# The attention stage of a one-core transformer kernel: new orders of the instructions on TensorE, VectorE, ScalarE, GpSimd and of the spreads

## The reference

```python
x = x + attn_a(_layernorm(x), ...)   # the stage that is changed
x = x + moe(_layernorm(x), ...)      # top 2 of 8 experts
x = x + gated_recurrence(_layernorm(x), ...)
x = x + moe(_layernorm(x), ...)

def attn_a(x):                        # 16 heads of 8, S = 256
    q, k, v = split(layernorm(x) @ in_proj_w.T + in_proj_b)
    scores = q @ k.T / sqrt(8) + causal_bias(rel_pos)
    x = x + (softmax(scores) @ v) @ out_w.T + out_b
    return x + relu(layernorm(x) @ w1.T + b1) @ w2.T + b2
```

## Time and profile before

| | |
|---|---|
| Three runs, median (lowest to highest) | 1711.88 us (1706.98 to 1714.66) |
| The profiled execution, its span | 1713.82 us, 1712.1 us |
| Busy over the span: PE, DVE, ACT, POOL | 1262.9, 1140.9, 965.3, 998.9 us |
| Mean granted TensorE clock (1 is 2.4 GHz) | 0.873 |

### The profile page before, as it was taken

The page is one execution under the profiler, slowest core; times in us unless marked ns, Lnnn a source line. Parts: engine busy times, 40 slices in busy tenths (PEclk is TensorE's granted clock), DMA queues, the critical chain, the costliest instruction groups (busy, mean ns, idle before and its releaser), DMA issues. The chain is left out here.

```text
span 1712.1 us, 37950 instructions
## 1 busy us (share of the span) xinstructions
PE 1262.9 (74%) x11717; PEld 1039.7 (61%) x11717; DVE 1140.9 (67%) x3828; ACT 965.3 (56%) x2002; POOL 998.9 (58%) x1152
## 2 busy tenths in 40 slices
PE   4688888888888888887458878747766628888750
PEld 2456666666666666665357878735554518878750
DVE  5377777777777777776555555548888735656548
ACT  2487877777777777775144444336666524444420
POOL 4234567767667667666745555534888845555450
PEclk8599999998999999988678998969899859999985
DMA  7121011111111111110332222211222122222218
GB/s 201 53 66 41 33 43 52 47 52 52 44 49 50 48 54 53 46 37 22 127 85 78 78 76 72 74 54 52 78 83 79 45 80 73 75 76 82 73 55 288
DMA packets 100818, 120.94 MB, mean 71 GB/s; under 512 B 17944, under 2 KB 80720, under 8 KB 100368
## 3 DMA queue, kind: packets, MB, share of 16 engines
q1 hardware_dynamic: 69600, 75.85, 14.9%
q0 software_dynamic: 17280, 35.95, 6.2%
q10 hardware_dynamic: 13744, 6.75, 1.4%
HBM read 49.45 MB, written 44.46 MB: 55 GB/s over the span
## 5 line engine op out<-in xcount | busy, mean ns | idle before, releaser
L1096 DVE TENSOR_TENSOR ebuf<-score_banks,region 128x768 f32<-128x768 f32 x256 | 243.9, 953 | 150.2 <-PE score_banks L809 143.7
L1333 ACT ACTIVATE region<-ebuf 128x768 f32<-128x768 f32 x256 | 216.9, 847 | 38.9 <-DVE ebuf L1096 34.8
L1311 ACT CAST copied<-max_banks 128x768 bf16<-128x768 f32 x256 | 204.7, 800 | 58.8 <-PE max_banks L797 55.8
L1745 POOL DMA_INDIRECT choice_rows<-first_yo,first_xg x142 | 137.3, 967 | 130.3 <-DVE first_yo L1865 96.3
L1745 POOL DMA_INDIRECT choice_rows<-second_yo,second_xg x142 | 137.1, 965 | 126.5 <-DVE second_yo L1865 92.3
L2161 POOL DMA_INDIRECT expert_rows<-d_rows,z_d_index x128 | 130.0, 1016 | 39.2 <-issue 31.9
L1614 POOL DMA_INDIRECT expert_rows<-d_rows,a_d_index x128 | 135.8, 1061 | 27.0 <-issue 21.3
L1821 ACT ACTIVATE first_silu<-first_bgu,first_biases 128x256 f32<-128x256 f32 x142 | 63.3, 477 | 130.1 <-PE first_bgu L1774 50.9
L1821 ACT ACTIVATE second_silu<-second_bgu,second_biases 128x256 f32<-128x256 f32 x142 | 62.9, 477 | 129.6 <-issue 52.2
L774 PE MATMUL max_banks<-identb,region 128*128 128x128 bf16 x512 | 109.8, 236 | 18.9 <-ACT copied L1311 17.7
L1857 DVE SCALAR_TENSOR_TENSOR first_hT<-first_bgu,first_biases,first_silu 128x256 f32<-128x256 f32 x142 | 64.3, 478 | 81.3 <-ACT first_silu L1821 49.1
(11 more groups left out here) (333 smaller groups left out, 4487.7 us busy)
## 6 DMA issues: line engine op xcount, KB each, us to landing
region_r<-region_r SPq DMA_DIRECT2D x192, 128.0 KB
first_xg<-expert_rows SPq DMA_DIRECT2D x71, 132.0 KB
second_xg<-expert_rows SPq DMA_DIRECT2D x71, 132.0 KB
z_rows<-choice_rows SPq DMA_DIRECT2D x32, 256.0 KB
c_rows<-choice_rows SPq DMA_DIRECT2D x16, 512.0 KB
out<-xres ACTq DMA_DIRECT2D x16, 256.0 KB
choice_rows<-first_yo,first_xg POOLq DMA_INDIRECT x142
choice_rows<-second_yo,second_xg POOLq DMA_INDIRECT x142
```

Of the source, the lines that this page charges most:

```text
L1096: nc.vector.tensor_tensor(ebuf[:, half_of_ebuf(c, j), :, :], score_banks[:, :, 0:BK], bias32[:, plain(j), :], ALU.add).then_inc(scores_fre ...
L1311: nc.scalar.copy(copied[:, 2 * j:2 * j + 2, :], max_banks[:, :, 0:BK]).then_inc(maxed_free, 1)
L1333: nc.scalar.activation(p32[:, j % 4, :, :], ebuf[:, half_of_ebuf(c, j), :, :], ACT.Exp).then_inc(exped, 1)
L1745: pool.indirect_dma_start(choice_dram, bass.IndirectOffsetOnAxis(ap=xg[:, i % G, t, E:E + 1].bitcast(I32), axis=0), yo[:, i % 4, t, :], No ...
```

## The change

No operation is added, removed or resized. The calls in the five body functions stand in another order, and some of them work on another batch in a given body: on DVE the third fold, masks 5 to 7, and the second norm of a batch now open the next body, on ACT exponentials 6 and 7, on POOL row_apply, the second root, second_apply, residuals, normed and normed_input come one body later and the roots one body earlier in the numbering. FIRST goes from -3 to -4 for that. In W_USES rank comes ahead of up. The DVE function second_norm is split into second_sum and second_norm; waits of DVE for its own statistics move from the end of one function to the start of the next (marks). On SP spread_projected is split into the upper and the lower parts of q and k, so q's are issued before k's. The diff, without the renamed arguments and the calls of body:

```diff
-    FIRST, FULL = -3, 8
+    FIRST, FULL = -4, 8
     T_USES = {"xmT": 2, "ot": 1, "up": 2, "row": 4, "oT": 1, "max": -1, "project": -3}
-    W_USES = {"project": -2, "ot": 1, "up": 2, "router": 4, "norm": -3, "rank": 5, "att": 1, "down": 2}
+    W_USES = {"project": -2, "ot": 1, "rank": 5, "up": 2, "router": 4, "norm": -3, "att": 1, "down": 2}
...
-            def body(b, n):
-                after, before = (n + 1) % RING, (n - 1) % RING
-                fill(b, n, 0, b + 1, after, 3)
-                weigh(b - 1, before, 3)
+            def body(b):
+                fill(b, b % RING, 0, b + 1, (b + 1) % RING, 3)
                 mlp_down(b - 3, 1)
-                fill(b, n, 1, b + 1, after, 4)
+                weigh(b - 1, (b - 1) % RING, 3)
+                fill(b, b % RING, 1, b + 1, (b + 1) % RING, 4)
+                project_kv(b + 2)
                 mlp_T(b - 2)
-                project_kv(b + 2)
-                fill(b, n, 2, b + 1, after, 5)
+                fill(b, b % RING, 2, b + 1, (b + 1) % RING, 5)
                 turn(b - 1)
-                fill(b, n, 3, b + 1, after, 6)
+                fill(b, b % RING, 3, b + 1, (b + 1) % RING, 6)
+                weigh(b, b % RING, 0)
+                rank(b - 5)
                 mlp_up_1(b - 2)
+                fill(b, b % RING, 4, b + 1, (b + 1) % RING, 7)
                 mlp_up_0(b - 2)
-                fill(b, n, 4, b + 1, after, 7)
                 row_T(b - 4)
-                weigh(b, n, 0)
+                fill(b, b % RING, 5, b + 2, (b + 2) % RING, 0)
                 router(b - 4)
-                fill(b, n, 5, b + 2, before, 0)
                 out_T(b - 1)
+                weigh(b, b % RING, 1)
                 norm_T(b + 3)
-                weigh(b, n, 1)
-                rank(b - 5)
-                fill(b, n, 6, b + 2, before, 1)
+                fill(b, b % RING, 6, b + 2, (b + 2) % RING, 1)
                 out_proj(b - 1)
-                max_T(b + 1, after)
+                max_T(b + 1)
+                weigh(b, b % RING, 2)
+                fill(b, b % RING, 7, b + 2, (b + 2) % RING, 2)
+                mlp_down(b - 2, 0)
                 project_q(b + 3)
-                fill(b, n, 7, b + 2, before, 2)
-                weigh(b, n, 2)
-                mlp_down(b - 2, 0)
 
...
-                    ch.mark(nc.vector.bn_stats(stats[:, t, :], tile(c, t)))
-                ch.wait(ch.base + ch.n)
+                    marks["norm"] = ch.mark(nc.vector.bn_stats(stats[:, t, :], tile(c, t)))
...
-            def second_norm(c, n):
+            def second_sum(c, n):
...
+
+            def second_norm(c):
+                if not exists(c):
+                    return
                 dve.wait_ge(W_free, useW("att", c) + 1)
                 for t in range(2):
-                    last = ch.mark(nc.vector.bn_stats(stats2[:, t, :], y1[:, t, :]))
-                ch.wait(last)
+                    marks["second"] = ch.mark(nc.vector.bn_stats(stats2[:, t, :], y1[:, t, :]))
...
+                ch.wait(marks["second"])
...
-            def body(b, n):
-                after, before = (n + 1) % RING, (n - 1) % RING
+            def body(b):
+                fold_keys(b, 2)
+                fold_half(b, 2)
+                fold_on(b, P // 4)
+                add_mask(b - 1, 5)
+                fold_on(b, P // 8)
+                sort(b - 5)
+                reduce_max(b, P // 8)
+                number(b - 5)
+                add_mask(b - 1, 6)
+                second_sum(b - 2, (b - 2) % RING)
+                second_norm(b - 2)
+                second_moments(b - 2)
+                add_mask(b - 1, 7)
+                fold_keys(b + 1, 0)
+                pick(b - 5)
+                take_q(b + 2)
+                fold_half(b + 1, 0)
                 add_mask(b, 0)
-                fold_keys(b + 1, 0)
                 finish(b - 3)
-                fold_half(b + 1, 0)
+                members(b - 5)
+                row_stats(b - 3)
                 add_mask(b, 1)
-                norm_stats(b + 3)
+                row_moments(b - 3)
                 take_low_xm(b - 2)
-                sort(b - 5)
                 take_k(b + 2)
                 add_mask(b, 2)
-                norm_moments(b + 3, n)
-                row_stats(b - 3)
+                norm_stats(b + 4)
+                normalise(b - 1)
                 add_mask(b, 3)
-                normalise(b - 1)
-                number(b - 5)
-                add_mask(b, 4)
+                place_a(b - 5)
                 fold_keys(b + 1, 1)
-                row_moments(b - 3)
-                pick(b - 5)
-                fold_half(b + 1, 1)
-                members(b - 5)
-                fold_keys(b + 1, 2)
-                fold_half(b + 1, 2)
-                add_mask(b, 5)
-                fold_on(b + 1, P // 4)
-                place_a(b - 5)
-                fold_on(b + 1, P // 8)
-                reduce_max(b + 1, P // 8)
-                add_mask(b, 6)
-                second_norm(b - 1, before)
-                second_moments(b - 1)
-                take_q(b + 3)
-                add_mask(b, 7)
+                norm_moments(b + 4, (b + 4) % RING)
                 place_b(b - 5)
                 place_c(b - 5)
+                fold_half(b + 1, 1)
                 place_d(b - 5)
+                add_mask(b, 4)
...
             def body(b):
+                exponentials(b - 1, 6)
+                copy_for_max(b + 1, 2)
+                take_upper_q(b + 2)
+                exponentials(b - 1, 7)
                 copy_for_max(b + 1, 3)
-                take_O(b - 1, 1)
                 exponentials(b, 0)
                 copy_for_max(b + 1, 4)
+                take_values(b + 2)
                 take_xmT(b - 2)
-                take_values(b + 2)
                 take_upper_k(b + 2)
+                take_O(b - 1, 1)
+                copy_for_max(b + 1, 5)
                 exponentials(b, 1)
-                copy_for_max(b + 1, 5)
                 exponentials(b, 2)
                 copy_for_max(b + 1, 6)
                 take_up_1(b - 2)
+                copy_for_max(b + 1, 7)
                 take_up_0(b - 2)
+                take_rowT(b - 4)
                 exponentials(b, 3)
-                take_rowT(b - 4)
-                copy_for_max(b + 1, 7)
+                copy_for_max(b + 2, 0)
+                take_logits(b - 4)
                 exponentials(b, 4)
-                take_logits(b - 4)
-                copy_for_max(b + 2, 0)
                 take_oT(b - 1)
                 take_norm(b + 3)
                 exponentials(b, 5)
-                take_O(b, 0)
                 copy_for_max(b + 2, 1)
                 take_max(b + 1)
-                exponentials(b, 6)
-                take_upper_q(b + 3)
-                copy_for_max(b + 2, 2)
-                exponentials(b, 7)
+                take_O(b, 0)
...
+            def spread_upper(c, n, part):
+                if not exists(c):
+                    return
+
+                if part == 0 and some(c - RING + 1):
                     sp.wait_ge(scores_full, 8 * (c - RING + 1))
-                for part in range(2):
-                    sp.wait_ge(hi_ready, 2 * c + 1 + part)
-                    for slot in UPPER[part]:
-                        spread_slot(n, hi, part, slot)
-                sp.dma_start(qs[n][SLOTS - 1:P:LANE // 2, :, :].bitcast(F32), zeros[:]).then_inc(spread, 16)
-                sp.wait_ge(T_free, useT("project", c) + 1)
-                spread_slot(n, lo, 0, LOWER[0])
-                sp.wait_ge(W_free, useW("project", c) + 1)
-                spread_slot(n, lo, 1, LOWER[1])
+                sp.wait_ge(hi_ready, 2 * c + 1 + part)
+                for slot in UPPER[part]:
+                    spread_slot(n, hi, part, slot)
+                if part == 0:
+                    sp.dma_start(qs[n][SLOTS - 1:P:LANE // 2, :, :].bitcast(F32), zeros[:]).then_inc(spread, 16)
+
+            def spread_lower(c, n, part):
+                if not exists(c):
+                    return
+                if part == 0:
+                    sp.wait_ge(T_free, useT("project", c) + 1)
+                else:
+                    sp.wait_ge(W_free, useW("project", c) + 1)
+                spread_slot(n, lo, part, LOWER[part])
...
-            def body(b, n):
-                after, before = (n + 1) % RING, (n - 1) % RING
-                spread_projected(b + 2, before)
-                spread_max(b + 1, after)
+            def body(b):
+                spread_upper(b + 2, (b + 2) % RING, 0)
+                spread_lower(b + 2, (b + 2) % RING, 0)
+                spread_upper(b + 2, (b + 2) % RING, 1)
+                spread_lower(b + 2, (b + 2) % RING, 1)
+                spread_max(b + 1, (b + 1) % RING)
...
-            def body(b, n):
-                after, before = (n + 1) % RING, (n - 1) % RING
-                roots(b + 3, n)
-                norm_apply(b + 3, n)
+            def body(b):
                 scatter(b - 6, 0, 2)
```

(28 more changed lines are left out.)

4 lines of the change are left out of this document (1 added, 3 removed).

## The result

The new orders take 1631.28 us (median of 4, 1625.22 to 1631.85) against 1713.27 beside them (4 runs, 1706.98 to 1715.83): a ratio of 0.952 [0.948, 0.955].

A forecast was written before the change was run, and what follows sets the result against it. No engine was full; PE, nearest to full, stood in three false waits, 3.16 us of a 23.36 us body. Removed, less new waits, 2.2 a body was won: 28 x 2.2 = 61.6 us, giving 1650 us, range 1626 to 1692.

The forecast's parts named there:

- Three false waits: On PE: L920 for normalised output 1.83, project_q for copied maxima 0.71, max_T for reduce_max 0.62; all 3.16 us a body go.
- The turn wait: PE's turn (L865) waits for take_O, which ACT does behind other copies: a new 0.7 us a body.
- norm_T waits 0.5 for the logits: PE's norm_T waits for its bank, which ACT's copy of the logits frees: a new 0.5 us a body.
- The walk: One body followed round its engines from the start of fill F3; closes at 20.9 us, 21.5 by differences, 21.2 taken.
- The clock, put at 0: PE's low clock in the MLP behind the gap: up to 1.3 us a body to win, 0 taken as cover.
- clock stays full: Rival: the low clock goes with the long gap, 2.2 + 1.0 = 3.2 us a body, 1622 us; chance 0.13.
- POOL, 1.2 us of cover: POOL's queue from the roots to xm for mlp_T takes 13.4 of 14.6 us, so 1.2 us to spare.
- the slower rival: POOL far late with xm, mlp_T waits every body: 1.8 us a body slower than now, 1762 us; chance 0.06.
- the small POOL rival: Ten POOL instructions each pay 0.27 us more, mlp_T 1.5 late: 0.7 us a body is left, 1692 us; chance 0.09.
- ACT becomes the chain: From F1 to F3 ACT's queue slips, PE waits 1.4 at turn, 1.1 at norm_T: 0.9 a body left, 1687; chance 0.12.
- it does nothing: Rival: PE's own stream of weight loads and matmuls sets the pace and waits only move: 1712 us; chance 0.05.
- Spreads and drain at 0: SP's spreads stay hidden (0, or 0.5 lost); POOL's drain of scatters is unchanged, 0 within 10 us either way.

The follow-up runs named there:

- normalise alone: The kernel before with one line moved: DVE normalises the attention output ahead of mask 3 instead of behind it; 20.75 us a body, ratio 0.956.
- the mended kernel: The changed kernel with POOL's normed between the second and third scatter and the fourth scatter behind the second norm's apply; 19.25 us a body, ratio 0.933 to before.
- Scatters apart: The changed kernel with POOL's normed ahead of the third scatter and normed_input ahead of the fourth; 20.11 us a body, ratio 0.952 to before.
- the same two edits: Normalise put back behind mask 3, or project_q right behind max_T: 20.30 and 20.28 us a body in the changed kernel, 20.31 and 20.31 with POOL's order mended.
- The first and the third series: Two of three series of four kernels, each beside the kernel before: first, filler, normalise moved, both put-backs in the changed kernel; third, the four with POOL's order mended.

## Why the prediction was right, and where it was off

- **Three false waits, 3.16 a body.** Right: they are gone. Two are shown to count: normalise alone won 2.61 in the kernel before, and in the mended kernel normalise and project_q each cost 1.06 when put back. The place of max_T's wait was not tried apart. The sum took the weight loads' waits; the matmuls', 2.67, are 0.5 less.
- **Their successors.** The turn wait was forecast at 0.7, released by take_O, and is 0.65. The 0.1 of the masks is not to be told from nothing.
- **norm_T waits 0.5 for the logits.** Wrong in kind: L736 is not among the matmuls' waits, and its weight loads wait 0.2 a body (5.4 us, 27 times). What came was 0.95 at the next user of that bank, out_proj, through the late copy of norm_T. The walk had the copy on time and nothing in the rows of before showed it late, as no three scatters stand in a row beside norm_T there.
- **The walk's 20.9 to 21.5, taken as 21.2.** Without the clock the change gave 3.17 - 1.29 = 1.88 a body (taking the two as additive) where 2.2 was forecast. The mended kernel, which has no wait at L889, gives 23.36 - 19.25 - 1.29 = 2.82, more than even the walk had (23.36 - 20.9 = 2.46).
- **The clock, put at 0.** This is the term that was mis-sized: it is 1.29 a body, 36 us in 28 bodies, the upper end of the 1.3 that the prediction names. The low end was taken as cover for waits that the walk misses, and such a wait came, 0.95. That is why 1650 was 19 us above the 1631 measured and no more: two errors of opposite sign, and their cancelling was luck. Without the held updates behind the 0.95 the kernel would have gained some 4.1 a body, as the mended one did (23.36 - 19.25), 115 us in 28 bodies: about 1597 (an estimate), below the range of 1626 to 1692. The rival "clock stays full" forecast 3.2 a body (measured 3.17) and 1622, and is the nearer one; my reason against it, that gaps of up to 0.7 us stay, does not hold: the gap of 0.66 ahead of turn stays and the clock with it, from 110 to 700 us:

```profile
110.00:700.00 590.00, 532.08 (x6977) 420.04 (x6977) 523.53 (x1437) 493.75 (x896) 434.58 (x571) 1.00 0.16 53
```

- **POOL, 1.2 us of cover.** Right only by luck: the chain left out that normed_input waits for second_sum (L1536 for L1119, 38.0 / 28 = 1.36 a body). xm still came late twice only. Scatters apart shows how thin the cover is: the mechanism of the slower rival then takes 0.56 a body. The price in the small POOL rival did not come: the scatters, which were to pay for the port pair that the Trainium skill describes (SBUF — State Buffer, "SBUF: two separate sides"), took a mean of 1031 ns from 150 to 700 us, against 1070 in the same stretch before. The 0.27 was itself a mean of two kinds: of the 48 instructions at L1594, the 24 beside DVE's L1074 took 1.30 and the other 24 took 0.84.
- **The rivals "ACT becomes the chain" and "it does nothing".** Neither came. ACT does set the turn wait, but at the 0.7 forecast and not at 1.4.
- **Spreads and drain at 0.** Right: where L800 is in the list of PE's waits (4.0 us in all, 13 times, 110 to 700 us), it is for DVE's L1096 and not for a DMA, and the time behind the last copy of the maxima is the same to 0.4 us.
- **The chances.** Those of the single cases add to 0.89 for faster and 0.06 for slower, where 0.88 and 0.07 are stated.

The line of after for the scatters over the whole kernel (busy us, mean ns, idle before):

```profile
L1625 POOL DMA_INDIRECT expert_rows<-d_rows,a_d_index x128 | 131.7, 1029 | 42.5 <-issue 30.8
```

## What to carry to other kernels

Look first for a wait of the busiest engine on a result that its next work does not need, and price the clock behind the gap as well as the gap: here one moved line won 2.61 us of 23.36, half of it clock. When an edit seems to cost nothing, check that its base ran beside it before concluding that its wait is off the path: the same two edits cost 0.1 us beside a kernel of another series and 1.06 beside one of their own. Code that no edit touches, here the 137 us behind the attention, tells that two series differ.

## What the runs showed of the hardware

- Work that nobody needs made the kernel faster: seven matmuls a body in the gap of 1.7 us kept the granted clock at its upper level, 2.4 GHz, and won 1.29 us a body.
- TensorE's semaphore updates can be held back while GpSimd issues indirect DMAs. In ten profiles 312 to 425 of its updates came over 0.3 us late; in the attention part all of these landed within 2.0 us of a scatter's start, the latest 2.4 us behind its instruction's end. With a third scatter in a row right beside norm_T, ScalarE stood idle 1.04 and 0.97 us for a transpose of 0.44, and restoring the third cost 0.88 us a body (19.25 to 20.13).
- In the four profiles of one series none was over 0.14 us late, with the same scatters in the same place, and the stages behind ran 137 us faster. The first and the third series ran on a chip of the same number, and the third had its updates held. What decides it is open.
